# A three-block transformer kernel on one core: the hand-written orders of all five engines made anew

## What is computed

```python
def _L0_ffn_ref(x, ...):
    h = jax.nn.silu(_tlin(x, w1_w, w1_s)) * _tlin(x, w2_w, w2_s)      # 128 -> 512
    h = jax.nn.gelu(_tlin(h, h1_w, h1_s), approximate=False)          # 512 -> 512
    h = jax.nn.gelu(_tlin(h, h2_w, h2_s), approximate=False)          # 512 -> 512
    return _tlin(h, w3_w, w3_s)                                       # 512 -> 128
...
x = x + 0.5 * _L0_ffn_ref(_layernorm(x), ...)
x = x + _L0_attn_ref(_layernorm(x), ...)   # exp of the logits, running sums over the sequence
x = x + 0.5 * _L0_ffn_ref(_layernorm(x), ...)
```

## Time and profile before

| | |
|---|---|
| median of 3 runs | 367.36 us (366.85 to 367.74) |
| span of the profiled execution | 366.2 us, 5192 instructions |
| PE busy | 359.0 us (98%), 1572 matmuls |
| weight loads (PEld) | 284.6 us (78%) |
| DVE busy | 319.5 us (87%) |
| ACT busy | 283.6 us (77%) |
| POOL busy | 171.9 us (47%) |
| chain that ended last | PE 97%, DVE 1% |

### The profile page before, as it was taken

The page is one execution under the profiler, slowest core; times in us unless marked ns, Lnnn a source line. Parts: engine busy times, 40 slices in busy tenths (PEclk is TensorE's granted clock), DMA queues, the critical chain, the costliest instruction groups (busy, mean ns, idle before and its releaser), DMA issues.

```text
span 366.2 us, 5192 instructions
## 1 busy us (share of the span) xinstructions
PE 359.0 (98%) x1572; PEld 284.6 (78%) x1572; DVE 319.5 (87%) x542; ACT 283.6 (77%) x463; POOL 171.9 (47%) x259
## 2 busy tenths in 40 slices
PE   7999999999999999999999999999999999999995
PEld 2678888778877887887878787887878877888885
DVE  5999788989989989999999989999999799947742
ACT  5898777886897789777876969868888796777763
POOL 3583375694124578512794545663574740520000
PEclk9999999999999999999999999999999999999999
DMA  7725504042000302100221021022024010050001
GB/s 255 242 96 167 166 2 115 0 113 62 1 2 0 99 18 58 59 4 0 56 63 57 3 58 59 0 59 58 0 60 117 1 57 2 0 143 2 30 1 59
DMA packets 17534, 21.44 MB, mean 59 GB/s; under 512 B 7392, under 2 KB 8672, under 8 KB 17248
## 3 DMA queue, kind: packets, MB, share of 16 engines
q1 hardware_dynamic: 16640, 20.15, 19.9%
q10 hardware_dynamic: 864, 0.93, 0.8%
HBM read 18.89 MB, written 2.19 MB: 58 GB/s over the span
## 4 chain that ended last, share of the span: by engine, by line
PE 97%; DVE 1%; ACT 0%; issue 0%; POOL 0%; POOLq 0%; DVEq 0%
PE hid_ps L654 62%; PE gate_ps L654 8%; PE y_ps L654 8%; PE up_ps L654 7%; PE y_ps L673 2%; PE xt_ps L847 2%; PE xt_ps L843 2%; PE xt_ps L850 2%; PE y_ps L763 1%; PE up_ps L718 1%; PE gate_ps L718 1%; DVE full L1092 0%; PE xt_ps L654 0%; DVE gate L1080 0%; DVE xt_sb L1152 0%
## 5 line engine op out<-in xcount | busy, mean ns | idle before, releaser
L654 PE MATMUL hid_ps<-act_hi,hi_h 128*128 128x512 f32 (+1 forms) x368 | 146.5, 398 | 0.0
L654 PE MATMUL hid_ps<-act_lo,hi_h 128*128 128x512 f32 (+1 forms) x368 | 143.1, 389 | 0.0
L1102 DVE TENSOR_TENSOR act_lo<-full,act_hi 128x512 fp32r<-128x512 f32 x157 | 117.3, 769 | 20.9 <-ACT act_hi L918 17.7
L911 ACT ACTIVATE full<-hid_ps,vec 128x512 f32<-128x512 f32 x123 | 84.3, 686 | 53.3 <-PE hid_ps L654 36.9
L654 PEld LDWEIGHTS hid_ps<-act_lo,hi_h 128*128 128x128 f32 x368 | 69.2, 188 | 16.3 <-issue 1.4
L654 PEld LDWEIGHTS hid_ps<-act_hi,hi_h 128*128 128x128 f32 x368 | 69.2, 188 | 16.0 <-issue 1.4
L918 ACT ACTIVATE act_hi<-full 128x512 fp32r<-128x512 f32 x127 | 78.6, 628 | 1.6
L580 POOL TENSOR_TENSOR xnt<-xt_sb,wide 128x512 f32<-128x512 f32 x22 | 31.6, 1437 | 49.5 <-DMA wide<-rows 43.8
L654 PE MATMUL hid_ps<-act_hi_second,hi_h 128*128 128x512 f32 x128 | 52.1, 407 | 0.0
L654 PE MATMUL hid_ps<-act_lo_second,hi_h 128*128 128x512 f32 x128 | 50.0, 390 | 0.0
L894 ACT ACTIVATE tanh<-gate_ps,s_half 128x512 f32<-128x512 f32 x60 | 40.6, 682 | 8.9 <-PE gate_ps L654 8.8
...
## 6 DMA issues: line engine op xcount, KB each, us to landing
...
```

The source lines that it names most:

```text
L654: mm = eng.matmul(ps, w, a, start=(first and n == 0), stop=(last and n == len(seq_) - 1))
L911: eng.activation(full23[m % 2][:, :], home23(n, T, m)[:, :], ACT.Gelu, scale=col("sh1" if n == 2 else "sh2", m)).then_inc(s_gelu[n], 1)
L1102: eng.tensor_tensor(act_lo[a][:, m, :], full[m % 2][:, :], act_hi[a][:, m, :].bitcast(F32), ALU.subtract).then_inc(s_lo[n], 1)
```

## The change

The lists of `START`, `SECOND_LAYER` and `STEPS` are written anew; every item of the old lists is in the new ones once, for the same tile, on the same engine. Nothing else in the file changes. Of 286 items on PE's lists 219 keep their place, of 436 on ACT's 209, of 441 on DVE's 235, of 87 on POOL's 69 and of 51 on SP's 42; most others move by one to three places. An item written at the end of a step instead of the start of the next, with its tile ahead of it, has not moved. The diff, cut to the opening and to the lists that the text below speaks of:

```diff
@@ -30,15 +30,16 @@
         "p1.0 p1.1 p1.2 flag:sum2 p1.3",
     ),
     "ACT": (
-        "hi:w1 bits:w2 hi:w2 z vec:s1 0:t bits:h1.1 bits:h1.3 0:tanh.0 0:tanh.1 0:tanh.2 0:high1.0 0:high1.1",
-        "bits:h2.0 bits:w3 tanh.3 high1.2 z.0 z.1 high1.3",
+        "bits:w2 hi:w1 hi:w2 z vec:s1 0:t bits:h1.1 0:tanh.0 bits:h1.3 0:tanh.1 bits:h2.0 0:tanh.2 0:high1.0 "
+        "0:high1.1",
+        "tanh.3 bits:w3 high1.2 z.0 z.1 high1.3",
     ),
     "DVE": (
         "stats aggr veps bits:w1 norm.0 norm.1 flag:copy1 norm.2 bits:h1.0",
-        "t vec:scales bits:h1.2 stats flag:raise2 gate.0 gate.1 up.0 flag:copy2 up.1 low1.0 aggr gate.2 veps "
-        "up.2 bits:h2.1 gate.3 up.3 2:stats low1.3 bits:h2.2 flag:raise3 1:t 3:stats flag:copy3 0:low2.0 "
-        "1:gate.0 0:low2.1 1:gate.1 1:up.0 1:up.1 0:low2.2 0:low2.3 1:low1.0 1:gate.2 1:low1.1 1:up.2 "
-        "1:gate.3 0:low3.0 2:t 1:up.3 1:low1.2 1:low1.3 0:low3.1 0:fold 0:low3.2",
+        "t bits:h1.2 vec:scales stats flag:raise2 gate.0 gate.1 flag:copy2 up.0 up.1 low1.0 aggr veps gate.2 "
+        "up.2 gate.3 up.3 bits:h2.1 2:stats low1.3 bits:h2.2 1:t flag:raise3 3:stats flag:copy3 0:low2.0 "
+        "1:gate.0 0:low2.1 1:gate.1 1:up.0 1:up.1 0:low2.2 0:low2.3 1:gate.2 1:low1.0 1:low1.1 1:gate.3 "
+        "1:up.2 1:up.3 0:low3.0 0:low3.1 2:t 1:low1.2 1:low1.3 0:low3.2 0:low3.3",
     ),
 }
 
...
-    "p2dhi.1 p2bhi.2 p2dlo.1 p2dhi.2 p2dhi.3 flag:sum3 p1.0 p2dlo.2 p2dlo.3 p1.1"
+    "p2dhi.1 p2bhi.2 p2dlo.1 p2dhi.2 p2dhi.3 flag:sum3 p1.0 p1.1 p2dlo.2 p2dlo.3"
...
+        "",
...
-        "hi:h2.0 hi:h2.1 norm hi:h2.2 hi:h2.3 3:norm xn.0 xn.1",
-        "hi:w3 xn.0 xn.1",
...
+        "hi:h2.0 hi:h2.1 norm 3:norm hi:h2.2",
+        "hi:h2.3 2:xn.0 2:xn.1 xn.0 hi:w3 xn.1",
...
-        "p1.0 p2.0 p2.1 p1.1 p2.2 p4 p2.3 p1.2 a3:u p1.3 a2:logits 8:u p3.0 p3.1 a2:keys 7:p1.0 p3.2 p3.3",
...
-        "a3:values p1.0 p1.1 p2.0 p2.1 p2.2 p1.2 p4 p2.3 p1.3 a5:u a4:logits p3.0 p3.1 a4:keys p3.2 p3.3",
-        "p1.0 p1.1 p4 p2.0 p2.1 u a4:values p2.2 p1.2 p2.3 a5:logits p1.3 12:u p3.0 a5:keys p3.1 p3.2 p3.3",
...
+        "4:p3.3 p2.0 p2.1 p4 p2.2 p2.3 a3:u p1.2 p1.3 a2:logits 8:u p3.0 p3.1 a2:keys p3.2 7:p1.0 7:p1.1",
...
+        "p1.0 p1.1 p2.0 p4 p2.1 u a3:logits a4:u p1.2 p2.2 p2.3 10:u a3:keys p1.3 p3.0 p3.1 p3.2 p3.3 "
...
+        "p2.0 p2.1 p2.2 p1.2 p4 p1.3 p2.3 a5:u a4:logits p3.0 p3.1 p3.2 a4:keys",
+        "8:p3.3 p1.0 p2.0 p1.1 p4 p2.1 u a4:values p2.2 p1.2 p2.3 p1.3 a5:logits 12:u p3.0 p3.1 a5:keys p3.2 "
...
-        "gelu2.0 gelu2.1 high2.0 high2.1 gelu2.2 high2.2 tanh.1 high1.0 a2:t gelu2.3 tanh.2 tanh.3 high1.1 "
-        "high2.3 a2:logits 7:t gelu3.0 a2:keys gelu3.1 high1.2 high3.0 high1.3 7:tanh.0 high3.1 gelu3.2 "
-        "high3.2 7:tanh.1 gelu3.3 high3.3",
...
-        "tanh.0 tanh.1 7:gelu3.3 7:high3.3 gelu2.0 high1.0 high2.0 gelu2.1 tanh.2 gelu2.2 a4:t high1.1 "
-        "high2.1 high2.2 gelu2.3 tanh.3 high2.3 a4:logits gelu3.0 high3.0 gelu3.1 high3.1 10:t gelu3.2 "
-        "high1.2 high3.2 high1.3 gelu3.3 high3.3",
...
-        "gelu2.0 gelu2.1 high2.0 high2.1 gelu2.2 high2.2 gelu2.3 high2.3 gelu3.0 high3.0 gelu3.1 high3.1 "
+        "bits:h2.3 t gelu2.0 high2.0 gelu2.1 tanh.0 high2.1 tanh.1 gelu2.2 gelu2.3 high2.2 high2.3 high1.0 "
+        "tanh.2 high1.1 gelu3.0 tanh.3 gelu3.1 high3.0 high3.1 2:t gelu3.2 high1.2 high3.2",
...
+        "gelu2.0 gelu2.1 high2.0 high2.1 tanh.1 gelu2.2 high2.2 a2:t gelu2.3 high1.0 tanh.2 tanh.3 high2.3 "
+        "7:t high1.1 a2:logits gelu3.0 a2:keys gelu3.1 high3.0 high3.1 high1.2 high1.3 7:tanh.0 gelu3.2 "
+        "high3.2 7:tanh.1",
...
+        "tanh.1 7:gelu3.3 gelu2.0 7:high3.3 high2.0 high1.0 gelu2.1 high2.1 tanh.2 gelu2.2 a4:t high2.2 "
+        "high1.1 gelu2.3 tanh.3 high2.3 a4:logits gelu3.0 gelu3.1 high3.0 high3.1 gelu3.2 10:t high3.2 "
+        "high1.2 high1.3 gelu3.3 high3.3",
...
+        "gelu2.0 gelu2.1 high2.0 high2.1 gelu2.2 gelu2.3 high2.2 high2.3 gelu3.0 high3.0 gelu3.1 high3.1 "
         "gelu3.2 high3.2 last:gelu.0 last:gelu.1",
...
-        "low3.3",
-        "gate.0 gate.1 up.0 low2.0 low2.1 up.1 dt gate.2 low1.0 a0:stats low2.2 low2.3 low1.1 up.2 3:t "
-        "4:stats gate.3 low1.2 up.3 low3.0 low1.3 low3.1",
...
-        "a1:weight_keys gate.0 4:low3.3 a1:pool up.0 low2.0 a1:values low2.1 dt gate.1 up.1 a3:stats low1.0 "
-        "low2.2 gate.2 low2.3 gate.3 up.2 7:t low1.1 8:stats up.3 a2:cumsum low3.0 low1.2 low3.1 low1.3 "
-        "low3.2",
...
-        "gate.0 a3:recip.1 up.0 gate.1 a3:weight_keys 7:low3.3 a3:pool low2.0 up.1 low1.0 dt low2.1 a3:values "
-        "gate.2 a5:stats low2.2 low2.3 gate.3 low1.1 up.2 up.3 a4:cumsum low3.0 a4:recip.0 10:t low3.1 low1.2 "
+        "",
+        "gate.0 up.0 0:fold low2.0 low2.1 gate.1 dt up.1 low1.0 gate.2 a0:stats low2.2 low2.3 low1.1 up.2 3:t "
+        "4:stats gate.3 low1.2 up.3 low3.0 low3.1 low3.2",
...
+        "5:low1.3 4:low3.2 4:low3.3 a1:weight_keys a1:pool gate.0 dt low2.0 low2.1 up.0 gate.1 up.1 a1:values "
+        "a3:stats low1.0 low2.2 low2.3 gate.2 7:t gate.3 low1.1 up.2 up.3 8:stats low3.0 low1.2 low1.3 "
+        "a2:cumsum low3.1",
...
+        "gate.0 a3:recip.1 up.0 gate.1 7:low3.3 low2.0 a3:weight_keys up.1 a3:pool low1.0 dt low2.1 a3:values "
+        "gate.2 a5:stats low2.2 low2.3 gate.3 low1.1 a4:cumsum up.2 up.3 low3.0 a4:recip.0 10:t low3.1 low1.2 "
         "low1.3 low3.2 low3.3",
```

More of the change, by code:

```diff
@@ L52 @@
     "SP": (
[L53 to L56, removed]
+        "park wide 3:park",
+        "wide",
+        "a0:park a0:wide park wide a1:park",
+        "a1:wide park wide",
         "park wide",
         "a2:park park a2:wide wide",
-        "a3:park a3:wide park wide",
-        "park wide",
+        "a3:park a3:wide park",
+        "8:wide park wide",
         "a4:park a4:wide park wide",
@@ L63 @@
         "park wide",
[L64 to L68, removed]
+        "a6:park a6:wide 8:store park wide",
+        "a7:park 9:store a7:wide park",
+        "10:store 14:wide park 11:store wide",
+        "12:store store 14:store",
+        "",
     ),
     "POOL": (
-        "hi:h2.0 hi:h2.1 norm hi:h2.2 hi:h2.3 3:norm xn.0 xn.1",
-        "hi:w3 xn.0 xn.1",
[L73 to L84, removed]
+        "hi:h2.0 hi:h2.1 norm 3:norm hi:h2.2",
+        "hi:h2.3 2:xn.0 2:xn.1 xn.0 hi:w3 xn.1",
+        "a0:norm norm a0:xn.0 a0:xn.1 xn.0 xn.1 a1:norm 5:norm",
+        "a1:xn.0 a1:xn.1 xn.0 xn.1 6:norm a0:weight",
+        "a0:dt xn.0 a1:weight xn.1 a2:norm",
+        "norm a2:xn.0 a2:xn.1 xn.0 xn.1",
+        "a3:norm a1:dt a2:weight norm a3:xn.0",
+        "a3:xn.1 8:xn.0 8:xn.1 a2:dt norm a4:norm a3:weight xn.0 xn.1 10:norm",
+        "a4:xn.0 a4:xn.1 xn.0",
+        "10:xn.1 a5:norm a4:weight a3:dt a5:xn.0 a5:xn.1 norm a4:dt xn.0",
+        "11:xn.1 norm a5:weight xn.0 xn.1",
+        "a6:norm a6:xn.0 a6:xn.1 a5:dt norm a6:weight a7:norm xn.0",
+        "13:xn.1 a6:dt a7:xn.0 a7:xn.1 norm xn.0 xn.1 a7:weight",
+        "a7:dt norm",
         "",
-        "",
+        "15:xn.0 15:xn.1",
     ),
```

## The result

The new kernel takes 377.59 us (median of four runs, 375.29 to 379.45), the kernel before on the same chip 367.55: 1.0277 times as long, with an interval of 1.0230 to 1.0324. That is 10.0 us slower where 1.9 were forecast.

The account below looks back on a forecast made before the run. PE was taken as the bound, busy 320.00 of 320.00 us from 30 to 350. The terms 0.66 + 0.8 + 0.5 = 1.96 were added to 367.36, giving 369.3 us, range 368.2 to 370.4 (367.3 to 370.9 with the rivals).

Parts of the forecast that it names:

- The variance pair: Opening, DVE: veps ahead of gate.2 is held by GpSimd's subtraction and delays gate.2; cost 0.66 us, bounds -0.3 and 1.0.
- Tile 2's low part: Step 0, DVE: up.3 and low3.1 now stand ahead of it, so PE gets it late; cost 0.4 us, bounds 0 and 0.8.
- Tile 6's up.0: Step 5, DVE: now behind dt and two subtractions, so up.1 ends late for PE's p1.3; 0.4 us, bounds 0 and 1.3.
- Step 5, p3.2 without cover: Step 5, PE: 7:p1.0 moves behind p3.2, which then waits for gelu3.0; cost 0.15 us, bounds 0 and 0.6.
- Step 8: PE: two fillers ahead of p3.2 go while ACT's 5.90 us chain stays; cost 0.8 us, bounds 0.5 and 1.1.
- The sign it gave: Around 207 to 208 us, PE's only new wait of about 1 us, for ACT's `full`.
- All other moves: Rest of the five lists, stores and flag copies: busy time hides them; cost 0, bounds -0.3 and +1.0 us.
- a long wait as a sign of being wrong: Steps 10 to 15: no long wait of PE was seen there, so any would show the prediction wrong.
- Counting three places at half: Between 30 and 140 us, terms 0.4, 0.4 and 0.15 counted as 0.5, since one delay gives others room.
- The opening won nothing: Rival: the variance pair slips in before POOL's subtraction, PE gains 0.3 to 0.9 before 22 us; 366.5 to 367.0, chance 0.10.
- the chain in step 8 wasn't shorter: Rival of no difference: opening costs about 0.5, step 8's chain is shorter than held; 367.3 to 367.9 us, chance 0.20.
- More is lost: Rival: subtractions meeting POOL take 1.5 to 1.7 us, also in steps 5, 9 and 12; 1.5 more, 370.8 us, chance 0.15.

Follow-up runs that it names:

- e12_again: The new kernel once more, unchanged, in a second set of five runs: 377.10 us, 1.026 times the kernel before.
- e4_cumsum_behind: The new kernel with 3:low1.3 and 2:low3.2 moved ahead of a0:cumsum on DVE, nothing else: 377.78 us, 1.0282 times the kernel before.
- e6_narrow_new: New kernel with narrow passes: GpSimd's four kinds of full-width passes cut to 8 of 512 columns from the third use on; 371.35 us, 1.0103.
- e13_small_fill: New kernel with GpSimd's passes cut to 8 of 512 columns and seven 2-column additions in front of each: 371.49 us, 1.0118.
- e16_up_first: New kernel with one item of DVE's step 5 moved, 6:up.0 ahead of low2.0 instead of behind low2.1: 377.04 us, 1.0292.

## Why the prediction was wrong

Its sign and its reading of the old kernel held: PE was full, so a new order had little to win and much to lose. The size was off by a factor of five, 1.96 us forecast and 10.0 measured. By its own steps, with the losses of `e12_again`'s column, where no fall of the clock is mixed in:

- *The variance pair, 0.66.* Right. Alone it costs 0.6 us; the whole opening 0.8. In the new kernel neg_mean starts at 14.78 and takes 1.13 us, and the chunk-2 product starts at 18.07 where the earlier trace rows has 16.97; p3.0 of tile 0 starts at 27.74 (forecast 27.5).

```profile
14.78 1.13 DVE L1073 TENSOR_SCALAR neg_mean<-mv 128x4 f32<-128x4 f32 x1
...
15.89 0.67 DVE L1088 SCALAR_TENSOR_TENSOR gate<-tanh,hid_ps 128x512 f32<-128x512 f32 x1
```

- *Tile 2's low part, 0.4.* It didn't come in the two traces of the new kernel. In four others with the same opening (`e4_cumsum_behind`, `e6_narrow_new`, `e13_small_fill`, `e16_up_first`) PE loses 0.3 us there, within the bounds.
- *Tile 6's up.0, 0.4.* Right in kind, mis-sized: 1.9 us are lost between the third layers of tiles 4 and 5. The step took the durations of the earlier trace rows, 1.49 and 1.12 us, from a place where the subtractions met GpSimd otherwise. In the new kernel each starts 0.3 us behind the start of one of GpSimd's passes, and they take 1.59 and 1.78 us, 3.29 together. And PE waits twice, at 6:p1.2 for up.0 and then at 6:p1.3 for up.1, where the step had the second wait alone:

```profile
134.54 3.29 DVE L1110 TENSOR_TENSOR act_lo<-full,act_hi 128x512 fp32r<-128x512 f32 x2
137.75 0.74 DVE L1100 SCALAR_TENSOR_TENSOR full<-up_ps,s_half,gate 128x512 f32<-128x512 f32 x1
```

```profile
138.55 0.50 PE L662 MATMUL gate_ps<-xn_hi,hi_w 128*128 128x512 f32 x1 [0.61 <-DVE full L1100]
```

- *Step 5, p3.2 without cover, 0.15.* 0.30 to 0.33 in every trace that has PE's and ACT's new lists there.
- *Step 8, 0.8.* Right: 0.87 alone. In the new kernel 1.46 are lost between the third layers of tiles 7 and 9, 0.79 with narrow passes, so DVE adds the rest. The sign it gave, one new wait of about 1 us for ACT's `full`, comes with narrow passes (0.87 us); in the full kernel that wait is 0.40, and one of 0.7 for DVE's `adelta` stands before it.
- *All other moves, 0, bounds -0.3 to +1.0.* This is the step that failed. The places it covers lose 1.1 us between 2:p3.0 and 3:p3.0 (3.8 in the run with the fallen clock), 0.2 from there to 4:p3.0, 0.5 in steps 6 and 7, 1.6 from 9:p3.0 to 11:p3.0 and 1.2 from there to 14:p3.0: 4.6 in all, where the step had 0 and at most 1.0. With narrow passes the same places lose 0.12 + 0.20 + 0.50 + 0.23 + 0.01 = 1.1 us. (Another 0.2 goes in step 1, at 1:p3.0, with full and with narrow passes.) So the step's rule, that an engine's busy time hides a change among items that are all needed later, was nearly right for the instructions' own length and wrong for their length beside GpSimd. Steps 10 to 12 show it, where the prediction found every reader served and named a long wait as a sign of being wrong: PE waits for DVE by 0.46, 0.32 and 0.45 us, and by nothing with narrow passes. In step 10 the running sum meets GpSimd's pass of 237.92 to 239.57:

```profile
237.81 2.30 DVE L1171 TENSOR_TENSOR_SCAN csum<-ones,kw 128x256 f32<-128x256 f32 x2
240.62 1.13 DVE L1110 TENSOR_TENSOR act_lo<-full,act_hi 128x512 fp32r<-128x512 f32 x1
...
244.19 0.68 DVE L1145 TENSOR_TENSOR xn_lo<-xnt,xn_hi 128x512 fp32r<-128x512 f32 x1
```

```profile
244.93 0.50 PE L662 MATMUL gate_ps<-xn_lo,hi_w 128*128 128x512 f32 x1 [0.46 <-DVE xn_lo L1145]
```

- *Counting three places at half*, because a delay gives the others room, was wrong as well. Between 30 and 140 us PE only falls further behind, and nowhere is more than 0.3 us given back (in step 8, with narrow passes). A PE that comes later makes little room for the others, since what it waits for is itself started by PE's products; that is read from the lists and not shown by a run of its own.
- *The rivals.* The opening won nothing, and the chain in step 8 wasn't shorter. "More is lost" had the mechanism, a subtraction of 1.5 to 1.7 us in a wrong place, but counted it for three stages at 0.5 us each and for subtractions alone. It should have been the forecast, with a count over all sixteen steps.

The prediction weighed the page "SBUF — State Buffer" of the Trainium skill, section "Who interferes with whom", for the one small operation only; for steps 0 and 5 it took stretched subtractions from the rows, and for the other steps its rival alone (more is lost) had any. The same section says that a DVE instruction with two SBUF inputs contends with a GpSimd instruction that reads SBUF. The traces agree: the subtractions, `weight_keys` and the running sum (`ones` and `kw`) take up to 1.8 us where they start during such a pass, while the gates (one input from PSUM) stay at 0.6 to 0.7 us and the reciprocals (one input) at 1.70 to 1.75 beside the same passes. So each of the 60 passes, of 1.3 to 1.9 us, had to be laid against the new DVE list, and that wasn't done.
